# A Perceiver layer on one core: three low halves moved to VectorE, one weight cast to ScalarE, one context quarter to VectorE, new orders

## What is computed

```
q = (layernorm(x) @ Wq.T + bq);  k = ctx @ Wk.T + bk;  v = ctx @ Wv.T + bv     # 16 heads of 16
x = x + softmax(q k^T / sqrt(16)) v @ Wo.T + bo                                # 64 queries, 1601 keys, 16 batches
q, k, v = split(layernorm(x) @ Wqkv + bqkv);  q, k = rope(q, k)
x = x + softmax(q k^T / 4) v @ Wout + bout                                     # 64 rows attend to 64
t = layernorm(x);  e = argmax(t @ wg);  keep the first 128 rows of each expert
x = x + softmax(t @ wg)[e] * (t @ W[e].T + b[e])                               # for the rows kept
```

## Time and profile before

| | us |
|---|---|
| median of 3 runs | 708.67 (708.53 to 710.76) |
| the profiled execution | 709.23 |
| its span, first to last instruction | 707.1 |
| PE busy | 673.3 |
| DVE, POOL, ACT busy | 556.5, 555.8, 443.4 |

### The profile page before, as it was taken

How to read it: one execution, slowest core, us unless ns; L and a number is a source line. 1 busy time by engine, 2 the same in 40 slices (tenths; PEclk the granted TensorE clock), 3 DMA queues, 4 the chain that set the end, 5 groups by cost and what they waited for, 6 DMA issues and landing times.

```text
span 707.1 us, 21580 instructions
## 1 busy us (share of the span) xinstructions
PE 673.3 (95%) x8636; PEld 508.9 (72%) x8681; DVE 556.5 (79%) x1135; ACT 443.4 (63%) x884; POOL 555.8 (79%) x378
## 2 busy tenths in 40 slices
PE   4899999999999999999999999999999996999898
PEld 2547786868686868686768786878686884777674
DVE  5698787878787878686878777878687888788867
ACT  2546767676667666767566666667666684765830
POOL 7959998989899888889988698889896898233522
PEclk9999999999999999999999999999999997999999
DMA  9586155454545454445444545454543430000213
GB/s 314 133 233 198 33 122 168 102 162 91 161 110 156 99 175 95 145 108 159 95 151 97 167 104 158 98 163 104 168 101 109 100 120 2 1 2 8 91 61 96
DMA packets 45609, 84.18 MB, mean 119 GB/s; under 512 B 8668, under 2 KB 28420, under 8 KB 45508
## 3 DMA queue, kind: packets, MB, share of 16 engines
q1 hardware_dynamic: 43896, 80.13, 41.2%
q0 software_dynamic: 912, 2.14, 1.0%
q10 hardware_dynamic: 704, 0.55, 0.2%
HBM read 36.89 MB, written 6.55 MB: 61 GB/s over the span
## 4 chain that ended last, share of the span: by engine, by line
PE 82%; DVE 6%; DMA 5%; issue 3%; SPq 2%; ACT 1%; POOL 0%; ACTq 0%; DVEq 0%; POOLq 0%
PE ps_kv L814 17%; PE ps_kv L805 16%; PE ps_score L865 12%; PE ps_front L837 12%; PE ps_out L889 11%; DMA kstack<-khigh 3%; SPq L501 2%; PE ps_score L913 2%; PE ps_kv L913 2%; PE ps_front L913 1%; PE ps_kv L780 1%; DVE maxes L1496 1%; DMA wq_sb<-in_wqT 1%; PE ps_out L905 1%; DMA q_blocks<-qbd 1%
## 5 line engine op out<-in xcount | busy, mean ns | idle before, releaser
L635 POOL TENSOR_TENSOR plow<-prob 128x1024 bf16<-128x1024 f32 (+1 forms) x201 | 377.1, 1892 | 57.0 <-ACT prob L1233 50.0
L1496 DVE TENSOR_REDUCE maxes<-ps_front 128x1 f32<-128x512 f32 (+1 forms) x416 | 267.3, 665 | 64.7 <-PE ps_front L837 62.0
L1233 ACT ACTIVATE prob<-ps_score 128x512 f32<-128x512 f32 (+1 forms) x416 | 236.2, 597 | 82.0 <-PE ps_score L865 74.5
L865 PE MATMUL ps_score<-qstack,kstack 98*128 98x128 bf16 (+1 forms) x1664 | 152.1, 219 | 0.3 <-ACT prob L1233 0.2
L837 PE MATMUL ps_front<-kstack,qstack 96*128 96x512 bf16 (+1 forms) x512 | 146.1, 333 | 4.5 <-DMA kstack<-khigh 3.9
L865 PEld LDWEIGHTS ps_score<-qstack,kstack 98*128 98x128 bf16 (+1 forms) x1664 | 113.4, 98 | 30.9 <-ACT prob L1233 1.2
L889 PE MATMUL ps_out<-vstack,prob 128*128 128x65 bf16 (+1 forms) x1664 | 114.0, 194 | 6.6 <-DVE plow L1466 5.8
L814 PE MATMUL ps_kv<-w_hi,cbuf 128*128 128x256 bf16 (+1 forms) x402 | 109.6, 273 | 0.3 <-DVE vstack L1486 0.3
L814 PE MATMUL ps_kv<-w_hi,clow 128*128 128x256 bf16 (+1 forms) x402 | 109.5, 272 | 0.0
L814 PE MATMUL ps_kv<-w_lo,cbuf 128*128 128x256 bf16 (+1 forms) x402 | 109.4, 272 | 0.0
L889 PEld LDWEIGHTS ps_out<-vstack,prob 128*128 128x128 bf16 (+1 forms) x1664 | 91.8, 98 | 24.1 <-DVE plow L1466 6.3
(11 more groups left out here) (288 smaller groups left out, 863.9 us busy)
## 6 DMA issues: line engine op xcount, KB each, us to landing
kstack<-khigh SPq DMA_DIRECT2D x256, 100.1 KB, 2.2
cbuf<-in_ctxT SPq DMA_DIRECT2D x15, 1601.0 KB, 6.8
kstack<-klow SPq DMA_DIRECT2D x128, 100.1 KB, 2.2
qstack<-q_blocks SPq DMA_DIRECT2D x48, 64.0 KB, 2.1
q_blocks<-qbd SPq DMA_DIRECT2D x16, 128.0 KB, 2.0
cbuf<-in_weT SPq DMA_DIRECT2D x2, 1024.0 KB, 6.6
slot_x<-att_all SPq DMA_DIRECT2D x8, 128.0 KB, 6.6
vstack<-slot_x SPq DMA_DIRECT2D x4, 256.0 KB, 4.3
```

The source lines that it names most:

```text
L635: nc.gpsimd.tensor_tensor(plow[slot][0:n, :], prob[slot][0:n, :], p_high(slot, 0, HP * P)[0:n], ALU.subtract).then_inc(plow_gps, 1)
L865: mm = nc.tensor.matmul(ps_score[0:nn, h % NSB, j * P:(j + 1) * P], kstack[par][0:98, hp, n0:n0 + nn], qstack[par][0:98, q_at(hp), :], sta ...
L1233: nc.scalar.activation(prob[slot][0:nn, e * 512:e * 512 + 512], ps_score[0:nn, h % NSB, :], ACT.Exp)\
L1496: nc.vector.reduce_max(maxes[:, hp:hp + len(unit), n], ps[:, 0:len(unit) * nn].rearrange("p (h k) -> p h k", k=nn), AX.X).then_inc(m_free, 1)
```

## The change

In the last batch POOL makes the low halves of three chunks (3, 6 and 9) in place of six (1, 2, 3, 7, 8 and 9), and DVE of ten in place of seven. At the start ACT casts the key weights, DVE only subtracts; POOL makes three of the first context's four low quarters and DVE the fourth (rows 128 to 255, keys from 801 on) right after the weights; the waits and their counts follow. The `fold` step gets a wait on the query norms that are ahead of it in POOL's own order. All four letter lists are other ones: the counts of their letters are the same, but for p on DVE (7, now 10) and on POOL (201, now 198). The diff, the lists cut to their last lines:

```
 PE_PROGRAM = [
...
-     "mmsKsmmsKmsswwmwsmwswKmwmssKmssmKmwmwsmKmsmwswwsmwmKmwmswswwmmssKmsmswwwsmmsZmswwAwsAswwswwsOssOswws"
-     "swwswswsswwswswswwsswHswswHswsJswswsTJAVOTSVwwwwwSPPwwHwWJVA2PTPOoWSA2HOoJPhPVlHWTJVAS2ThoOSPPhlWlP2"
-     "PAHocWOJAV2OHToJhSHlhTlVJcVPPTSWSPP2WoP2PxohWlxgchxg2lxgocgFhFFlFFFcFFFFFF", 1),
...
+     "wwsmsKmsmsKwmmwsswmwwmswKwsmKmsmKmswsmmKmssmwwmwsmwswmsmKmwswsmwmsKmsmwswmsZmswwswsAwswwwwssOswsAwsww"
+     "ssOswswwswswsswwswssswwsHsswwsJHswwsTJAVOTSVwwwwwSPPwHwwWJVAP2PTOoWSA2HOoJPPhVTHlWVJS2AToOhSPPhlWPl2"
+     "PHAocWOJAV2OHToJhSHlhTlVJcVPTPSWSPP2Wo2PPxoxhWlxghcxglx2gcogFhFlFFFFcFFFFFF", 1),
 DVE_PROGRAM = [
-    ("jkKBKzKCKkKKKzKkmmmmmmKmmjmmKmKmmKmKmmKmKmKmKmmKmKmKmmKmKmKmmKzmmmKmkmmKmmKmKmmmKmmKmmmmmmmKmmKvKmmK"
...
-     "mKmmmmKamZpvXDGXDGppNpNaLpLTppTXDGMMUUNMUMLUvWTXDxGdWNMULgMXUDnGNxTLWadgTnMMUUxdXgDMnMUGUWN1L3xXWDGT"
...
+    ("jKKKkKBzKkzKKCKmmmmmkmKmmjmmKmKmmKmKzmmKmKmmKmKmmKKmmKmKmKmKmmKmmmKmKmmmmKmKmmmmmKmmKmmmmmKmmKvKmmKm"
...
+     "KmKmmmKmaZpvppppXDXGDNpGLpNTLppTpXDGMMUUNaMMULUWvTXDxGWdNMgMLUUnXDGTNxLadgWTnMMUxUdXgDMnMUGUWN1xL3WX"
 POOL_PROGRAM = [
...
-     "cppcppppqpcppppppcppcppcpppcpppppppcppccppppcpcppppppcppcpppppppppppppppppbbppprrtptpZbIprIbbrbbRtrb"
-     "tRRtrrsRrRsIIssstRtYRtYRgYgggg", 1),
...
+     "pcpcppppqpppppppcppcpccpppppcpppcppcpppcpppppcpppppppccpcpppppppppppppppppbbpprrtZbptrbIbtbIIbrRrRbt"
+     "tRrrRtrsRsIsttssRRYYRggggYg", 1),
...
-GPS_CHUNKS, LAST_GPS = list(range(NCH)), [1, 2, 3, 7, 8, 9]
+GPS_CHUNKS, LAST_GPS = list(range(NCH)), [3, 6, 9]
...
+        wk_high, clow_dve = sem("wk_high"), sem("clow_dve")
...
-            for quarter in range(4):
+            for quarter in range(3):
                 low_context(0, quarter)
...
+                pool.wait_ge(h0_rdy, norms_done)          # in fold()
...
-                pe.wait_ge(clow_done, 4 * b + low_quarters(u))
+                if low_quarters(u) == 2:
+                    pe.wait_ge(clow_done, 4 * b - (b > 0) + 2)
+                else:
+                    pe.wait_ge(clow_done, 4 * b + 3)
+                    pe.wait_ge(clow_dve, 1)
                 if b == 0:
-                    pe.wait_ge(w_rdy, 2 if u < KUNITS else 4)
+                    pe.wait_ge(w_rdy, 1 if u < KUNITS else 3)
...
+            act.wait_ge(ld_wk, 16)
+            nc.scalar.copy(w_hi[0][:, :, :], w_f[0][:, :, :]).then_inc(wk_high, 1)
...
-                dve.wait_ge(ld_wv if n else ld_wk, 16)
-                nc.vector.tensor_copy(w_hi[n][:, :, :], w_f[n][:, :, :]).then_inc(w_rdy, 1)
-                dve.wait_ge(w_rdy, 2 * n + 1)
+                if n:
+                    dve.wait_ge(ld_wv, 16)
+                    nc.vector.tensor_copy(w_hi[n][:, :, :], w_f[n][:, :, :]).then_inc(w_rdy, 1)
+                    dve.wait_ge(w_rdy, 2)
+                else:
+                    dve.wait_ge(wk_high, 1)
                 nc.vector.tensor_tensor(w_lo[n][:, :, :], w_f[n][:, :, :], w_hi[n][:, :, :], ALU.subtract)\
                     .then_inc(w_rdy, 1)
...
             weight_parts(0)
+            dve.wait_ge(c_loaded[0], 16)
+            nc.vector.tensor_tensor(clow[0][:, 1, SPLIT:SK], cbuf[0][:, 1, SPLIT:SK], c_high(0, 1, SPLIT, SK - SPLIT),
+                                    ALU.subtract).then_inc(clow_dve, 1)
```

More of the change, by code:

```diff
@@ L128 @@
 ]
 ACT_PROGRAM = [
[L130 to L138, removed]
+    ("KKgKKKKKKKKKKKKKKgKKKKKKKKKKKKRKKReKeeeeKeKeeKeeKeeeeeeKKeeeeeeKeeReeKReeeKeKeeKeeKeeKeKeeKeKeeeegeK"
+     "eKeeeKeKKeeRKRKeeeeKeeKeeKeKeeeKeeeKeeKeeKeeeKKeeKReKeKRKeeeKeKeeeKeKeeKKeeeKeKeeKeeKeeeegeeKeKeRKKR"
+     "KeeKeeKeKeeKeeeeKeKeeKeeeKeeKeeKeeeKKeeKKRKeRKeeKeKeeKeeKeKKeKeeKeeeeeKKeeegeKeKeeeKeKRKeRKeeeKeeeKe"
+     "KeeeKeeKeeKKeeeKeKeeKeKeKeeKKeRKReKeeeKeeKeKeeeKeKeeKeeKeeKeKeegeKeeKeeKeKRKeReKeeKeeKeKeeeKeeeKeKee"
+     "KeKeKeeKeKeeeKeeKRKeRKeeKeeeKeeeKeKeeKeeKeeKeeKKeeKeegeKKeeKKReKeRKeeeKKeeKeeeeeKeKeKeKeKeeeKKeeKeee"
+     "KeKeeKRKReeKeeKeeKeeeeeKeeKKeeKeKeKKeeegeKeeKeKKReKeReKeeKeeKeeKeeKeeeKeeKeeKeKeeKeeeKKeeKKeKReRKeee"
+     "KeKeeeKKeeeeKeeeeKeKKeeeKeeKeKeKeKKeKReeRKeeeKeeKeeKeeKeKeeeKeKeeeeeZKeeeKeReeReeeAeeeeeAeeeeeeeeeee"
+     "eeHeeeHeeBATVTBVEEPPHEEVA2PTPBAH2EEPfPHViBTV2ABTEEfPPifEEPi2PAHlAV2HBTffHiTiBElVEVPTPBEEPP2EE2PPxhfi"
+     "xylhfxyixl2yyfhil", 1),
@@ L597, in rotated, with fold @@
                 nc.gpsimd.tensor_tensor(dst[..., 8:DH], src[..., 8:DH], src[..., 0:DH:2], ALU.add).then_inc(wrot_rdy, 1)
-            def fold(n, contexts_done, values_done, chunks_done):
+            def fold(n, contexts_done, values_done, chunks_done, norms_done):
                 pool.wait_ge(clow_done, contexts_done)
+                pool.wait_ge(h0_rdy, norms_done)
                 wait(pool, v0_low, values_done)
@@ L720, in _ @@
             chunks, folds, roots = iter(GPS_LOW), iter(range(3 + KT)), iter(range(1, TILES))
-            contexts_done, values_done, chunks_done, values = 4, 0, 0, iter(range(KUNITS, NREAL))
+            contexts_done, values_done, chunks_done, norms_done, values = 3, 0, 0, 1, iter(range(KUNITS, NREAL))
             tiles = {kind: iter(range(TILES)) for kind in "btrRI"}
@@ L728, in _ @@
                 if letter == "f":
-                    fold(next(folds), contexts_done, values_done, chunks_done)
+                    fold(next(folds), contexts_done, values_done, chunks_done, norms_done)
                 if letter == "v":
@@ L734, in _ @@
                     query_norm(next(roots))
+                    norms_done += 1
                 if letter == "p":
```

51 lines of the change are left out of this document (26 added, 25 removed).

## The result

The changed kernel takes 702.08 us (median of 4 runs, 700.5 to 702.73) against 709.63 for the kernel before (median of 4, 708.53 to 710.76): a ratio of 0.9877, 95% interval 0.986 to 0.9894. This ratio, like all that follow, is the one on record for the runs; the quotient of the two medians is 0.9894, at the upper end of the interval, so the gain is 8.7 us by the ratio and 7.5 by the medians. The forecast was 703.3, in a range from 699.0 to 708.8. The profiled execution took 701.69 us, span 699.7.

A forecast was written before the change was run, and what follows sets the result against it. In the last batch's stage TensorE waited for VectorE low halves held up by GpSimd's reads, and its clock fell; elsewhere mostly its own work bound it. 709.23 - 5.4, other terms 0, gave 703.8 profiled, 703.3 median; range 699.0 to 708.8.

The forecast's parts named there:

- The walk: Last batch's stage, followed step by step along the new order on four engines: tile 0's first rotated transposes 6.6 us earlier.
- The allowance of 1.2 us for one more blocked low: Last batch's stage: 1.2 us taken off the gain because the walk lets no low be blocked by chance.
- the sign of being right: Last batch's stage: ten VectorE lows with a mean of 1.2 to 1.5 us.
- The small waits: TensorE in the last batch's stage: 3.0 us of new small waits in place of the long one.
- The sign of being wrong: Last batch's stage: the prediction is wrong if TensorE's idle time doesn't fall below 4 us.
- The start: Key weights' cast and moved context quarter: TensorE gains 0.7 to 0.9 us, not passed on; term 0, between -0.6 and +0.8.
- The middle, 0 between -1.5 and +1.5: Stretch with 5.2 us of idle TensorE, mostly key DMAs: new orders can win or lose some of it.
- The second part, 0 between -1.5 and +2: Stretch from 604 us on, 7.4 us idle: GpSimd has three low_experts earlier, ahead of roots that VectorE waits for.
- The shared door as bound: Last batch's stage: reads of VectorE and GpSimd stay the bound, stage shrinks by 2.0 us only, 706.6; chance 0.14.
- VectorE as bound: Last batch's stage: VectorE's line becomes the slower bound, net +2.8 us, 711.5, from a mean low of 2.12; chance 0.10.
- Given back later: After the stage: its gain is lost again, 4 to 5 us, in second part and middle under new orders, 708.0; chance 0.11.
- The whole 9.6: Last batch's stage: all 9.6 us come, or start and middle add to the forecast, 699.1; chance 0.07.

The follow-up runs named there:

- the run with only one order of GpSimd changed: Kernel before, with GpSimd clearing its rooms ahead of tile 0's second constant and the lows of chunks 7 and 8; 708.09 us, 0.9972.
- the kernel with the two waits mended: Changed kernel, GpSimd clearing rooms and making chunk 9's low ahead of tile 0's sum, VectorE making tile 1's rotation one low earlier; 700.15 us, 0.985.

## Why the prediction was right, step by step

- **Where the time goes.** Right: the stage of the last batch carries the gain; alone it brings 6.2 us, against 5.4 forecast. The whole came to 7.5 us for the profiled execution (709.23 to 701.69), 2.1 more than the sum.
- **The walk.** It put the first rotated transposes at 594.8; they came at 593.04, but 1.44 us of that lie ahead of the stage. In the stage itself they moved 6.9 us, against 6.6 by the walk. The allowance of 1.2 us for one more blocked low was not needed in the sum, though the blocking came: the mean low was 1.53 us where the walk had 1.35 and the sign of being right 1.2 to 1.5.
- **The small waits.** Right in size, 3.0 us foretold and 3.4 in the named waits of the stage, 3.70 with all idle time of TensorE, and wrong in place. (The sign of being wrong, idle time not under 4 us, was missed by 0.3.) I had 0.5 for tile 0's rows and 0.8 for chunk 7; they came for tile 1's rows (1.33) and its rotation (1.12). The step that failed is that the walk let only low halves block each other: it gave tile 1's normalised rows no delay from GpSimd's sum and clearing, where 589.50 shows 2.29 us instead of 0.41, and tile 1's rotation none from chunk 9's low, where two lows ahead of it took 4.42.
- **The clock.** Right: it no longer falls, 1.00 for the stage. The longest wait left there is 1.33 us. It need not be as long as 5 us for the clock to fall: the run with only one order of GpSimd changed has 0.60 behind a wait of 2.85.
- **The start.** Right in most rows: cast 0.62 (0.63 taken), the first key-query product at 29.16 (29 within 0.8), a longer wait ahead of it (1.44), none for the context's low half. The query rows came at 12.93, not at 13.65 or later, and GpSimd's three quarters ended at 12.76, not at about 13.4; the query blocks still left 0.5 later, where 0.3 was forecast. The quarter took 1.50 on VectorE, between its ends of 0.94 and 3.6. Worth alone: 0.9999, as the 0 forecast; in the changed kernel it is worth more, as the next point says.
- **The middle, 0 between -1.5 and +1.5.** The measured value, 1.44 ahead of the stage, is within the bounds, and executions of one order differ by about as much (1.4). But the bounds were too narrow for what stands there: undoing the start costs 4.4 us in the middle of the profiled execution. I had taken start and orders as terms that add; they don't. That both move the place of TensorE's program loads among SP's key issues is the likely reason; for the waits it is shown in one direction only. The forecast was not hurt, as the changed kernel has a good place, and that is luck: no term of the sum stood for it.
- **The second part, 0 between -1.5 and +2.** 0.96 given back, inside.
- **The rivals.** The shared door as bound (706.6) falls: the stage lost 6.9 us, not 2.0. VectorE as bound (711.5) falls: the mean low stayed under 2.12, and even thirteen lows on VectorE are no slower. Given back later (708.0): a fifth of its size. The whole 9.6 (699.1): not reached, though the kernel with the two waits mended comes within 1.1 us of it.

## What to carry to other kernels

When two engines share a way to their data, look beside each over-long instruction for what the other engine ran at that moment: an order that lets GpSimd's work which only writes run beside VectorE's urgent two-input reads was worth some 2 us here twice (the second time within the intervals). It doesn't free every operation: the normalised rows, with one large input, took 0.85 us beside memsets instead of 0.41. How many lows each engine has mattered less: ten on VectorE or all thirteen came out level. A change of no worth alone can be worth 3 to 4 us in combination, so undo parts of the final kernel, and don't only add them to the old one. Before a new order is credited with a gain of a few us, see whether the same gain comes from a few idle instructions elsewhere.

## What the runs showed of the hardware that I had not expected

- A packet of the instruction queue beside SP's key issues goes with one issue that takes 0.6 to 1.3 us longer (2.54 instead of 1.23 us for a pair at 295.84), and 120 more waits at the head of TensorE's program moved these places and won back 2.1 us of the median (705.35 to 703.21), and 4.4 us between the spans of the profiled executions (705.8, the slowest of its six, to 701.4). How the one holds up the other isn't shown.
- A small tensor_scalar operation of VectorE, which reads one large tile and not two, is also held up beside GpSimd, and by memsets too: 128x256 from 0.41 to 2.29 us beside a sum and the memsets that follow it, and to 0.85 beside memsets alone; one of 128x2 took 1.48 us at 11.30 beside GpSimd's quarters. Not every one is: one of 128x1 took 0.15 at 585.21, beside GpSimd's low that began at 583.78.
- GpSimd is held up in its turn: its low of 1.89 us took 2.87 beside two VectorE lows.
- TensorE's granted clock was 0.60 from 593.35 to 600.00 us in the run with only one order of GpSimd changed, behind an idle time of 2.85 us.
